# Rows x and buffer z held four times, the adjacency in a buffer of its own, and a new order of steps on every engine

## The reference

```
layer 0: n = LN(h)*gamma1+beta1; 8 heads of 32: softmax(n n^T / sqrt(32), masked by adj > 0) n; r = h + that
         y = LN(r)*gamma2+beta2;  out = r + gelu(y W1 + b1) W2 + b2
layer 1, 2: p = h W; 4 heads of 64: softmax_j(leaky(src_i + dst_j), masked by adj > 0) p     (graph attention)
layer 3: q, k, v = h Wq+bq, h Wk+bk, h Wv+bv; 4 heads of 64: softmax(q k^T / sqrt(64), masked by adj or i == j) v
         out = relu(that Wo + bo)
x = x + out
```

## Time and profile before

| | |
|---|---|
| median of three runs | 4450.2 us |
| the profiled execution's own time | 4449.35 us |
| its span, first to last instruction | 4447.6 us |
| TensorE, matmuls | 4095.6 us busy, 92% |
| VectorE | 3239.7 us busy, 73% |
| ScalarE | 2175.2 us busy, 49% |
| GpSimd | 509.4 us busy, 11% |
| mean granted TensorE clock | 0.979 |

### The profile page before, as it was taken

One profiled execution on the slowest core, in us unless ns is written; L12 is line 12 of the kernel. 1 busy time (PEld: TensorE's weight loads), 2 busy tenths in 40 slices (PEclk: granted clock), 3 DMA queues, 4 the chain that ended last, 5 costly groups with the idle time before them and its releaser, 6 DMA issues.

```text
span 4447.6 us, 59477 instructions
## 1 busy us (share of the span) xinstructions
PE 4095.6 (92%) x22852; PEld 1941.3 (44%) x22884; DVE 3239.7 (73%) x6985; ACT 2175.2 (49%) x3361; POOL 509.4 (11%) x469
## 2 busy tenths in 40 slices
PE   6799999999999999999999999999999999999996
PEld 2344444344444344444444444444443444443443
DVE  5587767787767887677877777877677876678854
ACT  3454445554455544455544455544455544455432
POOL 0011111111111111011111011111111111111100
PEclk9899999999999999999999999999999999999998
DMA  2012110111110111111111110121110111101100
GB/s 81 20 44 53 53 53 21 33 53 53 53 49 20 39 53 53 53 39 29 39 53 53 53 34 23 50 53 53 53 32 22 53 53 53 50 18 39 53 29 29
DMA packets 212315, 193.93 MB, mean 44 GB/s; under 512 B 144448, under 2 KB 179008, under 8 KB 203584
## 3 DMA queue, kind: packets, MB, share of 16 engines
q1 hardware_dynamic: 212032, 190.12, 15.1%
HBM read 138.95 MB, written 17.56 MB: 35 GB/s over the span
## 4 chain that ended last, share of the span: by engine, by line
PE 63%; DVE 30%; issue 2%; ACT 2%; DMA 2%; POOL 1%; SPq 0%; POOLq 0%; ACTq 0%; DVEq 0%
DVE PG L989 13%; PE M L397 10%; PE M L410 10%; PE S L496 5%; PE O L512 5%; PE M L463 5%; DVE PP L875 5%; DVE x L906 4%; PE M L421 4%; PE O L343 3%; PE S L330 3%; PE O L449 3%; PE M L474 3%; DVE st L830 2%; PE O L354 2%
## 5 line engine op out<-in xcount | busy, mean ns | idle before, releaser
L989 DVE SCALAR_TENSOR_TENSOR PG<-g,tcg,mT 128x512 f32<-128x512 f32 x1024 | 692.9, 744 | 9.0 <-PE O L453 5.4
L597 ACT ACTIVATE PP<-S,reach 128x1024 f32<-128x1024 f32 x512 | 542.2, 1110 | 304.3 <-PE S L330 137.2
L875 DVE TENSOR_TENSOR PP<-PP,mT 128x1024 f32<-128x1024 f32 x512 | 599.0, 1217 | 43.0 <-ACT PP L597 41.9
L449 PE MATMUL O<-PG,V 128*32 128x512 f32 x4096 | 576.7, 637 | 43.6 <-DVE PG L989 26.5
L951 DVE TENSOR_TENSOR x<-x,M 128x256 f32<-128x256 f32 x128 | 54.0, 422 | 677.2 <-PE M L410 677.2
L1098 POOL TENSOR_SCALAR ve<-mv 128x4 f32<-128x4 f32 x192 | 168.9, 880 | 3163.8 <-DVE mv L837 2938.1
L397 PE MATMUL M<-hT,W 128*128 128x512 f32 x1024 | 467.5, 605 | 12.5 <-DVE rd L1035 10.6
L410 PE MATMUL M<-W,H 128*128 128x256 f32 x2048 | 461.3, 378 | 0.0
L621 ACT ACTIVATE z<-x,nb,rs 128x256 f32<-128x256 f32 x384 | 209.8, 596 | 479.7 <-DVE nb L865 479.7
L410 PEld LDWEIGHTS M<-W,H 128*128 128x128 f32 x2048 | 377.2, 189 | 68.4 <-issue 10.6
L1018 DVE TENSOR_TENSOR PP<-PP,m 128x1024 f32<-128x1024 f32 x256 | 301.3, 1219 | 71.9 <-ACT PP L712 71.9
(11 more groups left out here) (136 smaller groups left out, 5551.3 us busy)
## 6 DMA issues: line engine op xcount, KB each, us to landing
g<-t_rows SPq DMA_DIRECT2D x64, 1024.0 KB, 5.6
g<-adj_in SPq DMA_DIRECT2D x32, 1024.0 KB, 6.7
x<-x_in SPq DMA_DIRECT2D x32, 512.0 KB, 5.1
z<-t_rows SPq DMA_DIRECT2D x64, 256.0 KB, 4.0
out<-x SPq DMA_DIRECT2D x32, 512.0 KB, 3.4
W<-w_in SPq DMA_DIRECT2D x1, 3072.0 KB, 16.6
mT<-V SPq DMA_TRANSPOSE x128, 2.6
m<-hT SPq DMA_TRANSPOSE x128, 2.5
```

The source lines that it names most:

```text
L449: e.matmul(k.O[0][r:r + 32, :], s.V[:, jt, 64 * hh + 32 * v:64 * hh + 32 * v + 32], p[:, u, :], start=(jt == 0), stop=(jt == NT - 1))
L597: e.activation(p[:, 2 * pair:2 * pair + 2, :], k.S[:, 2 * pair:2 * pair + 2, :], ACT.Exp, bias=k.reach[:, 7:8], scale=SC0).then_inc(k.e0.s ...
L875: e.tensor_tensor(p[:, 2 * pair:2 * pair + 2, :], p[:, 2 * pair:2 * pair + 2, :], s.mT[:, jt:jt + 1, :].to_broadcast([128, 2, N]), ALU.mul ...
L989: e.scalar_tensor_tensor(out=p[:, u, :], in0=s.T[hh], scalar=s.tcg[:, 1, hh, jt:jt + 1], in1=s.mT[:, jt, :], op0=ALU.max, op1=ALU.mult).th ...
```

## The change

`x` and `z` are held four times (`NX = 4`, set `b % 4`), the other buffers three times (`Both` puts a set together). The adjacency has one buffer for all batches, loaded again once both masks of the batch before are made. The first mask is written into `z`, the second into `V` (before: `V` and `hT`), so that `ln0` waits for the first mask's transposes (before: `ln1`), and `ln1` for the second's (before: `qt` on ScalarE). `rs` and `nb` of the first norm wait until the batch three before has its last `lnz`. SyncE's `load` is split in `loada` (adjacency) and `load` (rows). The loop is cut at another place: a turn works on b1 = it-1 (masks, norms, first scores), b2, b3, b4, in the orders below. Lines of the form `e, k, s = ...`, in which every step now asks `self.k.of(b)` for its set, are left out.

```diff
--- before.py
+++ after.py
+NX = 4
...
-        return self.sems[b % NS]
+        return self.sems[b % self.n]
     def at(self, b):
-        return self.sems[b % NS], 16 * self.per * (b // NS + 1)
+        return self.sems[b % self.n], 16 * self.per * (b // self.n + 1)
...
+        self.adj = sb("adj", [128, NT, N], I32)
+        self.xz = []
+        for k in range(NX):
+            s = Set()
+            s.x = sb(f"x{k}", [128, NT, D])
+            s.z = sb(f"z{k}", [128, NT, D])
+            s.tr = s.z[0:16, 0, 0:128]
+            s.sq = s.z[:, 0:2, :].rearrange("p t d -> p (t d)").bitcast(BF16).rearrange("p (c n) -> p c n", c=2)
+            s.rb = s.z[:, :, :].rearrange("p t d -> p (t d)").rearrange("p (c n) -> p c n", c=2)
+            s.mk = s.z[:, :, :].rearrange("p t d -> p (t d)").bitcast(BF16).rearrange("p (t n) -> p t n", t=NT)
+            self.xz.append(s)
...
-            s.adj = s.g[:, :, :].bitcast(I32)
-            s.mk = [s.V[:, :, :].rearrange("p t d -> p (t d)").bitcast(BF16).rearrange("p (t n) -> p t n", t=NT),
-                    s.hT[:, :, :].rearrange("p c n -> p (c n)").bitcast(BF16).rearrange("p (t n) -> p t n", t=NT)]
+            s.mk = s.V[:, :, :].rearrange("p t d -> p (t d)").bitcast(BF16).rearrange("p (t n) -> p t n", t=NT)
...
+        self.sets = [Both(self.rest[b % NS], self.xz[b % NX]) for b in range(NS * NX)]
...
     def ln0(self, b, t):
...
         self.wait_ge(*k.nb[0].at(b, 0))
-        if b >= NS:
-            self.wait_ge(*k.woa.at(b - NS, 1))
+        self.wait_ge(*k.lm[0].at(b))
         e.activation(s.z[:, t, :], s.x[:, t, :], ACT.Relu, bias=s.nb[:, t:t + 1],
...
     def ln1(self, b, t):
...
         self.wait_ge(*k.nb[1].at(b, 0))
-        self.wait_ge(*k.lm[0].at(b))
+        self.wait_ge(*k.lm[1].at(b))
         e.activation(s.V[:, t, :], s.z[:, t, :], ACT.Identity, bias=s.nb[:, t:t + 1],
                      scale=s.rs[:, t:t + 1]).then_inc(k.v0.sem, 1)
...
     def out0(self, b, q):
...
         self.wait_ge(*k.pv0.at(b, 4 * q + 3))
-        self.wait_ge(*k.mk.at(b, 1))
+        if b >= NS:
+            self.wait_ge(*k.o3.at(b - NS, 0))
         e.activation(s.OT[q], k.O[0][:, :], ACT.Copy, scale=k.w("g1c")[:, q:q + 1]).then_inc(k.oc0.sem, 1)
...
     def masks(self, b, which):
...
         self.wait_ge(*k.la.at(b))
-        if b >= NS:
-            self.wait_ge(*(k.wo.at(b - NS, 1) if which else k.pv3.at(b - NS, 3)))
-        e.tensor_scalar(s.mk[which][:, :, :], s.adj, 0.0, None, ALU.not_equal if which else ALU.is_gt).then_inc(k.mk.sem, 1)
+        if which and b >= NS:
+            self.wait_ge(*k.pv3.at(b - NS, 3))
+        if not which and b >= NX:
+            self.wait_ge(*k.o3.at(b - NX, 0))
+        e.tensor_scalar(s.mk[which][:, :, :], k.adj[:, :, :], 0.0, None, ALU.not_equal if which else ALU.is_gt).then_inc(k.mk.sem, 1)
...
     def nb(self, b, i):
...
+        if i == 0 and b >= NS:
+            self.wait_ge(*k.zr[3].at(b - NS, 3))
         if i == 1:
             self.wait_ge(*k.z0.at(b, 3))
         self.wait_ge(*k.rs[i].at(b, 0))
...
     def rs(self, b, i):
...
         self.wait_ge(k.consts, NCONST)
         self.wait_ge(*k.stat[i].at(b, 0))
+        if i == 0 and b >= NS:
+            self.wait_ge(*k.zr[3].at(b - NS, 3))
         c = self.chained(e.tensor_scalar(s.ve[:, :], s.mv[:, :, 1], EPS, None, ALU.add))
         self.wait_ge(*c)
...
     def load_adj(self, b):
...
-        if b >= NS:
-            self.wait_ge(*k.o3.at(b - NS, 0))
-        e.dma_start(s.adj, k.adj_d[b].rearrange("(t p) j -> p t j", p=128)).then_inc(k.la.of(b), 16)
...
+        if b:
+            self.wait_ge(*k.mk.at(b - 1, 1))
+        e.dma_start(k.adj[:, :, :], k.adj_d[b].rearrange("(t p) j -> p t j", p=128)).then_inc(k.la.of(b), 16)
     def load_x(self, b):
...
-        if b >= NS:
-            self.wait_ge(*k.so.at(b - NS))
...
+        if b >= NX:
+            self.wait_ge(*k.so.at(b - NX))
         e.dma_start(s.x[:, :, :], k.x_d[b].rearrange("(t p) d -> p t d", p=128)).then_inc(k.lx.of(b), 16)
     @step
     def load(self, b):
         if b:
+            self.load_x(b)
+
+    @step
+    def loada(self, b):
+        if b:
             self.load_adj(b)
-            self.load_x(b)
...
-        self.wait_ge(*k.lm[1].at(b))
+        if b >= NS:
+            self.wait_ge(*k.wo.at(b - NS, 1))
...
-        if b >= NS:
-            self.wait_ge(*k.lw[2].at(b - NS))
...
 def tensor_program(do):
+    for it in range(1, NB + 4):
+        b1, b2, b3, b4 = it - 1, it - 2, it - 3, it - 4
+        do.b2r(b3, 1, 1)
+        do.pv0(b2, 0)
+        do.pv0(b2, 1)
+        do.dn0(b2, 0)
+        do.b2r(b3, 1, 2)
+        do.b2r(b3, 1, 3)
+        do.sc0(b2, 3)
+        do.pv0(b2, 2)
+        do.tt(b4, 3, 0)
+        do.tt(b4, 3, 1)
+        do.sc0(b2, 4)
+        do.qk(b4, 0)
+        do.qk(b4, 1)
+        do.pv0(b2, 3)
+        do.dn0(b2, 1)
+        do.sc0(b2, 5)
+        do.qk(b4, 2)
+        do.qk(b4, 3)
+        do.pv0(b2, 4)
+        do.pv0(b2, 5)
+        do.sq3(b4, 0)
+        do.sc0(b2, 6)
+        do.vp(b4, 0)
+        do.sc0(b2, 7)
+        do.vp(b4, 1)
+        do.dn0(b2, 2)
+        do.pv0(b2, 6)
+        do.pv0(b2, 7)
+        do.sq3(b4, 1)
+        do.dn0(b2, 3)
+        do.sc3(b4, 0)
+        do.tt(b3, 2, 0)
+        do.tt(b3, 2, 1)
+        do.sc3(b4, 1)
+        do.b2r(b2, 0, 0)
+        do.b2r(b2, 0, 1)
+        do.pv3(b4, 0)
+        do.sc3(b4, 2)
+        do.b2r(b2, 0, 2)
+        do.b2r(b2, 0, 3)
+        do.pv3(b4, 1)
+        do.pj(b3, 2, 0)
+        do.pj(b3, 2, 1)
+        do.pj(b3, 2, 2)
+        do.pj(b3, 2, 3)
+        do.sc3(b4, 3)
+        do.dn3(b4, 0)
+        do.prep_b(b2)
+        do.tt(b2, 0, 0)
+        do.tt(b2, 0, 1)
+        do.pv3(b4, 2)
+        do.w1(b2, 0)
+        do.w1(b2, 1)
+        do.pv3(b4, 3)
+        do.grow(b3, 2)
+        do.dn3(b4, 1)
+        do.w1(b2, 2)
+        do.w1(b2, 3)
+        do.w1(b2, 4)
+        do.w1(b2, 5)
+        do.w1(b2, 6)
+        do.w1(b2, 7)
+        do.den3(b4)
+        do.rd3(b4)
+        do.w2(b2, 0)
+        do.w2(b2, 1)
+        do.w2(b2, 2)
+        do.w2(b2, 3)
+        do.gpv(b3, 2, 0)
+        do.gpv(b3, 2, 1)
+        do.tt(b2, 1, 0)
+        do.tt(b2, 1, 1)
+        do.pj(b2, 1, 0)
+        do.pj(b2, 1, 1)
+        do.pj(b2, 1, 2)
+        do.pj(b2, 1, 3)
+        do.wo(b4, 0)
+        do.wo(b4, 1)
+        do.grow(b2, 1)
+        do.gpv(b3, 2, 2)
+        do.gpv(b3, 2, 3)
+        do.b2r(b3, 2, 0)
+        do.b2r(b3, 2, 1)
+        do.b2r(b3, 2, 2)
+        do.b2r(b3, 2, 3)
+        do.gpv(b2, 1, 0)
+        do.qt(b1, 0)
+        do.gpv(b2, 1, 1)
+        do.sc0(b1, 0)
+        do.gpv(b2, 1, 2)
+        do.sc0(b1, 1)
+        do.qt(b1, 1)
+        do.gpv(b2, 1, 3)
+        do.sc0(b1, 2)
+        do.b2r(b2, 1, 0)
...
 def scalar_program(do):
+    for it in range(1, NB + 4):
+        b1, b2, b3, b4 = it - 1, it - 2, it - 3, it - 4
+        do.sc0(b2, 3)
+        do.tt(b4, 3, 0)
+        do.tt(b4, 3, 1)
+        do.sc0(b2, 4)
+        do.qk(b4, 0)
+        do.out0(b2, 0)
+        do.qk(b4, 1)
+        do.sc0(b2, 5)
+        do.sq3(b4, 0)
+        do.qk(b4, 2)
+        do.qk(b4, 3)
+        do.sc0(b2, 6)
+        do.sc0(b2, 7)
+        do.sq3(b4, 1)
+        do.lnz(b3, 2, 0)
+        do.vp(b4, 0)
+        do.lnz(b3, 2, 1)
+        do.vp(b4, 1)
+        do.lnz(b3, 2, 2)
+        do.lnz(b3, 2, 3)
+        do.out0(b2, 1)
+        do.sc3(b4, 0)
+        do.tt(b3, 2, 0)
+        do.tt(b3, 2, 1)
+        do.sc3(b4, 1)
+        do.sc3(b4, 2)
+        do.pj(b3, 2, 0)
+        do.pj(b3, 2, 1)
+        do.pj(b3, 2, 2)
+        do.out3(b4, 0)
+        do.ln2(b2, 0)
+        do.ln2(b2, 1)
+        do.ln2(b2, 2)
+        do.pj(b3, 2, 3)
+        do.ln2(b2, 3)
+        do.tt(b2, 0, 0)
+        do.tt(b2, 0, 1)
+        do.sc3(b4, 3)
+        do.gprep(b3, 2)
+        do.w1(b2, 0)
+        do.w1(b2, 1)
+        do.grow(b3, 2)
+        do.w1(b2, 2)
+        do.w1(b2, 3)
+        do.out3(b4, 1)
+        do.w1(b2, 4)
+        do.w1(b2, 5)
+        do.ln0(b1, 0)
+        do.w1(b2, 6)
+        do.ln0(b1, 1)
+        do.w1(b2, 7)
+        do.ln0(b1, 2)
+        do.rd3(b4)
+        do.lnz(b2, 1, 0)
+        do.lnz(b2, 1, 1)
+        do.lnz(b2, 1, 2)
+        do.lnz(b2, 1, 3)
+        do.tt(b2, 1, 0)
+        do.tt(b2, 1, 1)
+        do.ln0(b1, 3)
+        do.pj(b2, 1, 0)
+        do.pj(b2, 1, 1)
+        do.gout(b3, 2, 0)
+        do.pj(b2, 1, 2)
+        do.pj(b2, 1, 3)
+        do.gprep(b2, 1)
+        do.grow(b2, 1)
+        do.gout(b3, 2, 1)
+        do.ln1(b1, 0)
+        do.ln1(b1, 1)
+        do.ln1(b1, 2)
+        do.ln1(b1, 3)
+        do.qt(b1, 0)
+        do.gout(b2, 1, 0)
+        do.sc0(b1, 0)
+        do.sc0(b1, 1)
+        do.qt(b1, 1)
+        do.gout(b2, 1, 1)
+        do.lnz(b3, 3, 0)
+        do.lnz(b3, 3, 1)
+        do.lnz(b3, 3, 2)
+        do.lnz(b3, 3, 3)
+        do.sc0(b1, 2)
...
 def vector_program(do):
+    for it in range(1, NB + 4):
+        b1, b2, b3, b4 = it - 1, it - 2, it - 3, it - 4
```

(165 more changed lines are left out.)

516 lines of the change are left out of this document (89 added, 427 removed).

## The result

The changed kernel takes **4386.64 us** (median of 4 runs, 4385.58 to 4388.06) where the kernel before took 4450.02 on the same chip; the ratio is 0.9858, 95% interval 0.9841 to 0.9875. The profiled execution's span is 4385.0 us against 4447.6. The forecast was 4389, within 4345 to 4450.

The account below looks back on a forecast made before the run. VectorE and TensorE were taken to bound the kernel by turns: 30.6 + 101.4 + 0.22 = 132.2 us a turn against 134.46, 64 us less over 29 turns; 4449.35 - 64 + 4 = 4389 us, range 4345 to 4450.

Parts of the forecast that it names:

- The bound, and the length of a turn: VectorE and TensorE alternate in setting the pace; a turn falls from 134.46 to 132.2 us, over 29 turns.
- VectorE part: Layer 2's first reciprocal to layer 3's second `tt`, VectorE full: 1.8 us of statistics and `nb` leave, 30.56 becomes 28.75 us.
- TensorE part: From layer 3's second `tt` to layer 2's last `gpv`: 99.05 us bare work plus waits, 101.4 us against 101.85.
- The new wait for the mask: `ln0` on ScalarE waits for the first mask's transposes, delaying the gelu that frees `den3`'s bank: 0.4 us a turn.
- the projections' 0.32: Layer 1's sixteen `pj` projections after the 0.73 us wait still take 0.32 us longer than unhindered.
- The lump of 0.4 for small waits: TensorE part: 0.4 us a turn added for unseen waits of 0.1 to 0.3 us.
- Root on GpSimd: Norm 3's `nb` waits 1.48 us with VectorE idle; if slow in norms 2 and 3, the sum is 23 us higher.
- Broadcast ahead of `gw(., 1, 0)`: Layer 2's end: the broadcast lands 2.9 us after the last `gpv`, `gw` comes at 3.8; no cost, 0.9 us spare.
- Start and end: Outside the full turns: start +9 us from later masks, end -5 us from a covered reciprocal broadcast, net +4.
- The gelus wait for the mask: Slower rival: slow transposes delay `ln0` and the gelus behind it; 136.3 us a turn, 4508 us; chance 0.10.
- What leaves the VectorE part comes back behind it: No-change rival: the 1.8 us are paid again at the first `sq3`; turn 134.0, 4440 to 4455 us; chance 0.08.
- More gain: Faster rival: `pj`'s 0.73 and 0.32 and the 0.4 of small waits vanish; 130.75 a turn, 4346 us; chance 0.08.

Follow-up runs that it names:

- The statistics' run: Changed kernel with norm 0's four `bst` and four `bag` moved back to the start of the VectorE-full stretch: 4441.27 us, ratio 0.9983 to the kernel before.
- the two runs with the statistics early: Changed kernel with norm 5's last `bag` before layer 1's last `gw`: 4382.91 us; the same plus the first mask's transposes ahead of layer 2's row: 4371.41 us.
- the run with the mask sooner: Changed kernel with the first mask's four transposes ahead of layer 2's row and broadcast on SyncE: 4411.6 us, ratio 0.9915 to the kernel before.

## Why the prediction was right

*The bound, and the length of a turn.* Right: 132.2 foreseen, 132.15 measured, so 67.1 us for 29 turns where 64 stood in the sum. That the two agree to 0.05 is partly luck. The prediction added 30.6 + 101.4 us of a turn and kept 0.22 for what the mean turn had beyond it. The turn in the windows takes 131.70, 0.3 less, and the mean has 0.45 beyond it: 0.32 for late masks, 0.10 for the slow turns of GpSimd, 0.03 of others. The prediction had the late mask in every turn instead, and nothing of the second.

*VectorE part.* Right: 28.75 against 28.82, and from the last `gpv` to the first reciprocal 1.85 us where 1.83 were carried over. The statistics' run gives the reason its weight: 1.64 us in the part are 1.57 a turn where neither a late mask nor a slow turn of GpSimd interferes.

*The fourth buffers worth nothing.* Right, measured alone.

*TensorE part.* 101.4 foreseen, 101.03 measured in a turn whose mask was not late, 0.32 more with the average of the late ones: right within its bounds, but with some terms against each other. As foreseen: `sq3` 0.16, `rd3` 0.35, `pj` 0.73, the 0.50 at `gpv` gone and that at `grow` down to 0.18. The new wait for the mask has the mechanism and the mean size foreseen, but not the form: 0.4 was taken for each turn, and the runs show nothing in 21 turns and 0.3 to 2.9 us in eight (0.32 on average in the changed kernel, 0.41 between the two runs with the statistics early). In the turn read the last transpose landed 10.6 us after `grow`, where 11.0 were worked out; where it costs nothing it lands a microsecond earlier. Wrong: the projections' 0.32 went (3.87 us for sixteen); why isn't shown. Not seen: 0.45 at `sc0(., 7)` and 0.44 at the second `sq3`, both behind ScalarE. The lump of 0.4 for small waits stood in for these and the 0.18, 1.07 together, so that term was a guess. In sum the waits of this turn are 2.31 us, with the mask's at nothing, where 2.36 were foreseen with the projections' 0.32 and the mask's 0.4 in them; the bare work is 98.7 us where 99.05 were carried over, and where that 0.3 went isn't shown.

*Root on GpSimd.* The mechanism was named, but at the wrong norm. At norm 3 `nb` waits 1.47 us, where 1.48 were taken. Norms 2 and 3 cost nothing on TensorE that the rows show. The place that counts is norm 5, which the prediction took as unchanged because its steps are in both lists. In the old order the two additions of `pa0` (2.34 us), two reciprocals and four small steps of `b2r` (0.86 us) lie between the last `bag` of norm 5 and its `nb`; the new order has four multiplications in an unbroken row there. The prediction compared the sets of steps of the VectorE part, and not what VectorE does between handing something to GpSimd and wanting it back. With 4.51 us in all turns the changed kernel would take 27 x 1.34 = 36 us more, some 4423 (an estimate from the turns of the run with the mask sooner), and still be faster than before. That it had it in only two turns was luck as far as the prediction goes.

On this the Trainium skill, page "SBUF — State Buffer", section "SBUF: two separate sides", says that VectorE's instruction with two SBUF inputs and GpSimd's that reads SBUF hold the shared ports for the whole instruction, and the later of the two is blocked until the first has finished. The trace agrees on the block and shows it to be longer: 4.51 us is not one multiplication of 1.15 but four in a row. Of 30 turns it was that in 2 or in 27, with the same start behind the first multiplication to within 0.03 us.

*Broadcast ahead of `gw(., 1, 0)`.* Its slack was put at 0.9 us. From the row to the broadcast 2.94 us had been taken from layer 2's; layer 1's took 1.40 (2109.58 to 2110.98), so the slack was about 2.4 us. Moving `grow` 2.6 us closer should then have cost 0.2 and cost 1.08, as the broadcast landed 6.0 us after its issue and not 5.0; what held it isn't shown.

*Start and end.* +9 and -5 foreseen, +9.4 and -4.9 measured. At the start `ln1` begins at 31.74 us where 31.2 were worked out, and the first exponential 8.8 us later than before where 7.5 were. At the end the wait of 9.38 us is gone; a new one of 3.02 us for a product, with slow matmuls behind it, wasn't foreseen.

*The signs.* Of those that would have shown it wrong, a granted clock below 1 in full turns came, 0.97 to 1.00; but the kernel before has it as well, so it told nothing. `ln0`'s idle time is 1.0 us in the mean, not about 2, and TensorE's wait at `den3`, foreseen as 0.5 us at most, reaches 0.96 in one turn.

*The rivals.* "The gelus wait for the mask" came in small, in eight turns, two of which took 134.38 and 134.58 us; with transposes some 4 us later it comes in all of them, and then costs 5.29 us a turn, not the wait alone. The prediction let it cost one for one; the clock behind the stall was missing, 1.6 us a turn there, and 1.7 us behind a stall of 0.75 in the changed kernel. "What leaves the VectorE part comes back behind it" did not: the first `sq3` keeps its 0.16. "More gain" came in one of its terms (0.32).

## What to carry over

Find the stretch in which one engine is full and the others wait, and move out of it every instruction that isn't needed there: it was worth nearly its full length here, 1.64 us of work for 1.57 us of turn, while buffers alone gave nothing and a buffer placed without its order cost 2%. When steps are reordered, compare not only which steps stand in the stretch, but what the consumer does between handing something to another engine and wanting it back; a chain over GpSimd beside VectorE needs room for its longest case, and one `bag` moved 2.7 us ahead was worth 40 us of 4411. Price a new stall of TensorE at its length plus what runs at the lower clock behind it. And look at the turns one by one before a mean is explained: a term of 0.3 us a turn was nothing in most turns and 2.7 us in a few.

## What the runs showed of the hardware

GpSimd's 128 x 4 instruction took 0.23 us alone and 1.11 or 4.51 us beside four multiplications of VectorE in a row, and 4.51 made the turn 1.34 us longer; four DMA transposes issued earlier by SyncE turned 28 fast turns of 30 into 3. After a PARTITION_ALL_REDUCE the next instruction of GpSimd starts 6.8 to 7.9 us later with nothing to wait for (48 of 64 times; 7.2 in the median):

```profile
2060.59 0.39 POOL L1136 PARTITION_ALL_REDUCE amx<-mx  x1 [6.19 <-DVE mx L991]
2068.11 0.25 POOL L1128 TENSOR_SCALAR ve<-mv 128x4 f32<-128x4 f32 x1 [7.14 <-issue]
...
2069.61 0.16 DVE L893 SCALAR_TENSOR_TENSOR nb<-mv,rs 128x4 f32<-128x4 f32 x1 [2.98 <-POOL rs L1130]
```

Here it costs VectorE 2.98 us that it has to spare, as it then waits 8.49 us for `den3`. The Trainium skill, page "GPSIMD Engine Reference", section 2.1 (Instruction dispatch), puts the first call after newly loaded code at some 6 us, with no instruction in the profile; the gap here may be of that kind, as a MODIFY_POOL_CONFIG stands at its start (2060.9), but it is a microsecond longer, and no run here shows what fills it.

The transposes of a mask on SyncE took 5.25 us to issue behind one broadcast, and 6.87 us behind a broadcast and the store of the result in the same turn.
